# One TensorE increment per round in the routed stage, with the down product a round later

## What is computed

```python
xn = _layernorm(x, axis=-1)
x = x + _L0_attn_ref(xn, ...) + _L0_ffn_ref(xn, ...)

# the experts: 16 of them, each row goes to 6; H = 256, I = 176
topk_idx, topk_weight = _gate(hs, gate_weight, bias)
comb = zeros((T, E)).at[arange(T)[:, None], topk_idx].add(topk_weight)
for e in range(E):
    g = hs @ gate_proj[e].T
    u = hs @ up_proj[e].T
    inter = silu(g) * u
    out = out + comb[:, e:e + 1] * (inter @ down_proj[e].T)
# and a shared expert that every row goes to
```

## Time and profile before

| | us |
|---|---|
| median of 3 timed runs | 474.18 |
| lowest and highest | 473.19, 474.95 |
| span of the profiled execution (its own time; no time around it is recorded) | 518.7 |
| TensorE, VectorE, ScalarE, GpSimd busy in it | 426.0, 359.5, 228.7, 225.0 |
| gate/up products, 444 records | 156.4 |
| down products, 444 records | 117.3 |

### The profile page before, as it was taken

One profiled execution on the slowest core, in us unless ns is written; L12 is line 12 of the kernel. 1 busy time (PEld: TensorE's weight loads), 2 busy tenths in 40 slices (PEclk: granted clock), 3 DMA queues, 4 the chain that ended last, 5 costly groups with the idle time before them and its releaser, 6 DMA issues.

```text
span 518.7 us, 7330 instructions
## 1 busy us (share of the span) xinstructions
PE 426.0 (82%) x1981; PEld 324.8 (63%) x1981; DVE 359.5 (69%) x582; ACT 228.7 (44%) x614; POOL 225.0 (43%) x221
## 2 busy tenths in 40 slices
PE   6699986984979899898998999994987299979800
PEld 5698875764846667676776777673755177657600
DVE  3548931288698889898999999995630055548961
ACT  3542423211754444644576656632652044624400
POOL 2700175665346667671000000074757624466662
PEclk8559988898999999999999999998997689988955
DMA  7999925564725556567732333364567454464473
GB/s 201 345 351 396 385 104 177 176 245 153 225 66 190 174 189 192 167 195 211 191 106 88 102 106 109 102 176 124 155 178 191 123 149 141 133 174 142 122 219 89
DMA packets 65957, 91.55 MB, mean 176 GB/s; under 512 B 8448, under 2 KB 57344, under 8 KB 65664
## 3 DMA queue, kind: packets, MB, share of 16 engines
q1 hardware_dynamic: 54144, 63.02, 39.6%
q0 software_dynamic: 9216, 25.96, 16.2%
q10 hardware_dynamic: 2560, 2.10, 1.5%
HBM read 43.48 MB, written 47.57 MB: 176 GB/s over the span
## 4 chain that ended last, share of the span: by engine, by line
PE 60%; DVE 12%; issue 10%; another core or an unknown queue 6%; ACT 5%; POOL 2%; DMA 2%; SPq 2%; DVEq 0%; POOLq 0%; ACTq 0%
PE gate L923 20%; PE ps_y L946 15%; PE ps_y L939 4%; PE up L913 4%; PE misc L822 3%; PE ps_y L882 3%; PE misc L793 2%; PE misc L973 2%; PE gate L860 2%; DVE prod L1021 2%; PE up L860 1%; SPq L402 1%; PE ps_y L822 1%; DVE inter_s L1432 1%
## 5 line engine op out<-in xcount | busy, mean ns | idle before, releaser
L923 PE MATMUL gate<-wrec,xgT 128*128 x444 | 156.4, 476 | 3.8 <-DVE inter_s L1432 2.7
L562 POOL DMA_INDIRECT xs_dram<-xrow,slot_i x96 | 105.5, 1099 | 72.1 <-DMA xs_dram<-xrow,slot_i 25.8
L946 PE MATMUL ps_y<-wrec,interT 88*128 x444 | 117.3, 387 | 0.1
L582 POOL DMA_INDIRECT gat<-y_dram,slot_i x50 | 54.1, 1083 | 141.5 <-DMA y_dram<-y_s 103.0
L1432 DVE SCALAR_TENSOR_TENSOR inter_s<-gate,xg,gate_s 128x176 f32<-128x176 f32 x111 | 43.6, 393 | 80.6 <-ACT gate_s L687 38.7
L923 PEld LDWEIGHTS gate<-wrec,xgT 128*128 128x128 f32 x444 | 78.5, 197 | 30.7 <-issue 7.9
L946 PEld LDWEIGHTS ps_y<-wrec,interT 88*128 88x128 f32 x444 | 76.8, 193 | 7.5 <-issue 0.9
L939 PE MATMUL ps_y<-ident,inter_s 128*88 128x128 f32 x222 | 43.1, 276 | 33.3 <-issue 16.1
L939 PEld LDWEIGHTS ps_y<-ident,inter_s 128*88 128x88 f32 x222 | 25.6, 124 | 70.9 <-issue 51.4
L707 ACT ACTIVATE y_s<-ps_y 128x256 f32<-128x256 f32 x108 | 41.4, 383 | 63.7 <-PE ps_y L946 39.2
L687 ACT ACTIVATE gate_s<-gate 128x176 f32<-128x176 f32 x111 | 35.5, 320 | 72.6 <-PE gate L923 52.1
(11 more groups left out here) (200 smaller groups left out, 666.6 us busy)
## 6 DMA issues: line engine op xcount, KB each, us to landing
xg<-xs_dram SPq DMA_DIRECT2D x111, 136.0 KB
y_dram<-y_s SPq DMA_DIRECT2D x111, 128.0 KB
xs_dram<-zrow SPq DMA_DIRECT2D x1, 9384.0 KB, 33.7
wrec<-wexp SPq DMA_DIRECT2D x14, 608.0 KB
xs_dram<-zrow SPq DMA_DIRECT2D x14, 408.0 KB
xn_dram<-xrow SPq DMA_DIRECT2D x8, 256.0 KB, 3.3
qkv<-xn_dram SPq DMA_DIRECT2D x8, 256.0 KB
xs_dram<-xrow,slot_i POOLq DMA_INDIRECT x96
```

Of the source, the lines that this page charges most:

```text
L562: nc.gpsimd.indirect_dma_start(xs_dram[0:DONE[max(d for d in DONE if d <= c)] * P, :], bass.IndirectOffsetOnAxis(slot_i[:, o:o + 1], 0), x ...
L582: nc.gpsimd.indirect_dma_start(places[place_of(n)][:, there:there + H], None, y_dram[0:DONE[max(d for d in DONE if d <= first)] * P, :], b ...
L923: last = nc.tensor.matmul(guA[t % 2][:, 0:2 * I], xgT[:, t % 2, k * P:(k + 1) * P], wrec[:, bass.ds(record + k * 2 * I, 2 * I)], start=(k ...
L946: last = nc.tensor.matmul(ps_y[:, t % 2 * 2 * H:t % 2 * 2 * H + H], interT[:, t % 2, k * P:(k + 1) * P], wrec[0:HALF, bass.ds(record + KT ...
```

## The change

TensorE's round is reordered to columns(t+2), down(t-4), middle(t-2), gate/up(t), and only the last instruction of the round increments a semaphore, the new `round_ps`. The down product is one round later; the results and their stores follow, so there is one more round. Everybody who waited for a piece waits for the end of the round in which it stands (`rounds`). The buffers' other waits change with the order: the middle transposes wait for the middle copy of two tiles before in place of the result copy, the down product waits for the result copy of two tiles before, and VectorE's `middle` no longer waits for TensorE's transposes.

```diff
+        def rounds(t, later):
+
+            return t + later + 3
...
-            for t in range(NT + 3):
+            for t in range(NT + 4):
                 if t + LEAD < NT:
                     load_tile(t + LEAD)
-                if t >= 3:
-                    store_tile(t - 3)
+                if t >= 4:
+                    store_tile(t - 4)
...
-                act.wait_ge(xt_ps, t + 1)
+                act.wait_ge(round_ps, rounds(t, -2))
...
-                act.wait_ge(gu_ps, t + 1)
+                act.wait_ge(round_ps, rounds(t, 0))
...
-                act.wait_ge(it_ps, t + 1)
+                act.wait_ge(round_ps, rounds(t, 2))
...
-                if t + 2 in EXP_AT and t:
-                    act.wait_ge(y_sb, t)
-                act.wait_ge(yt_ps, t + 1)
+                if t + 3 in EXP_AT:
+
+                    act.wait_ge(it_sb, t + 3)
+                    if t:
+                        act.wait_ge(y_sb, t)
+                act.wait_ge(round_ps, rounds(t, 4))
...
-                    pe.wait_ge(y_sb, t - 1)
+                    pe.wait_ge(it_sb, t - 1)
...
                 pe.wait_ge(it_sb, t + 1)
+                if t >= 2:
+
+                    pe.wait_ge(y_sb, t - 1)
...
-                    gate_up_tile(t, held[t])
+                if t + 2 < NT:
+                    last = columns(t + 2)
+                if t >= 4:
+                    last = down_tile(t - 4, held[t - 4])
                 if 2 <= t <= NT + 1:
-                    middle(t - 2)
-                if t >= 3:
-                    down_tile(t - 3, held[t - 3])
-                if t + 2 < NT:
-                    columns(t + 2)
+                    last = middle(t - 2)
+                if t < NT:
+                    last = gate_up_tile(t, held[t])
+
+                last.then_inc(round_ps, 1)
...
                 dve.wait_ge(gate_ok, t + 1)
-                if t >= 2:
-
-                    dve.wait_ge(it_ps, t - 1)
-
...
-                dve.wait_ge(yt_ps, t + 1)
+                dve.wait_ge(round_ps, rounds(t, 4))
+                dve.wait_ge(it_sb, t + 3)
...
                 if t in EXP_AT:
-                    if t >= 3:
-                        tile_result(t - 3)
+                    if t >= 4:
+                        tile_result(t - 4)
```

More of the change, by code:

```diff
@@ L317, in build @@
         d_ok, y_ok = sem("d_ok"), sem("y_ok")
-        xt_ps, xt_sb, gu_ps, gate_ok, mid_ok, it_ps, it_sb, yt_ps, y_sb = (
-            sem("xt_ps"), sem("xt_sb"), sem("gu_ps"), sem("gate_ok"), sem("mid_ok"), sem("it_ps"), sem("it_sb"),
-            sem("yt_ps"), sem("y_sb"))
+        round_ps, xt_sb, gate_ok, mid_ok, it_sb, y_sb = (
+            sem("round_ps"), sem("xt_sb"), sem("gate_ok"), sem("mid_ok"), sem("it_sb"), sem("y_sb"))
         step, sub_ok, exp_ok, att_ok, attx_ok = sem("step"), sem("sub_ok"), sem("exp_ok"), sem("att_ok"), sem("attx_ok")
@@ L758, in _ @@
                 else:
-                    if t >= 3:
-                        result(t - 3)
+                    if t >= 4:
+                        result(t - 4)
                     if t + 2 < NT:
@@ L913, in columns @@
                     last = nc.tensor.transpose(guB[t % 2][:, k * P:(k + 1) * P], xg[:, t % RING, k * P:(k + 1) * P], ident[:, :])
-                last.then_inc(xt_ps, 1)
+                return last
             def gate_up_tile(t, record):
@@ L924, in gate_up_tile @@
                                             wrec[:, bass.ds(record + k * 2 * I, 2 * I)], start=(k == 0), stop=(k == KT - 1))
-                last.then_inc(gu_ps, 1)
+                return last
             def middle(t):
@@ L939, in middle @@
                     last = nc.tensor.transpose(ps_y[0:HALF, o:o + P], inter_s[:, t % 2, k * HALF:(k + 1) * HALF], ident[:, :])
-                last.then_inc(it_ps, 1)
+                return last
             def down_tile(t, record):
                 pe.wait_ge(it_sb, t + 1)
+                if t >= 2:
+                    pe.wait_ge(y_sb, t - 1)
                 for k in range(2):
@@ L947, in down_tile @@
                                             wrec[0:HALF, bass.ds(record + KT * 2 * I + k * H, H)], start=(k == 0), stop=(k == 1))
-                last.then_inc(yt_ps, 1)
+                return last
             def transpose_attention(j):
@@ L982, in _ @@
                 qkv_job(n)
-            columns(0)
-            columns(1)
+            columns(0).then_inc(round_ps, 1)
+            columns(1).then_inc(round_ps, 1)
             pe.wait_ge(w_in, 16 * TAIL)
             pe.wait_ge(tail_in, 16)
-            for t in range(NT + 3):
+            for t in range(NT + 4):
                 if t < NT:
@@ L1437, in tile_columns @@
                 dve.wait_ge(xt_sb, t)
-                dve.wait_ge(xt_ps, t + 1)
+                dve.wait_ge(round_ps, rounds(t, -2))
                 nc.vector.tensor_copy(xgT[:, t % 2, :], guB[t % 2][:, 0:H]).then_inc(xt_sb, 1)
@@ L1444, in tile_middle @@
                     dve.wait_ge(it_sb, t)
-                dve.wait_ge(it_ps, t + 1)
+                dve.wait_ge(round_ps, rounds(t, 2))
                 nc.vector.tensor_copy(interT[:, t % 2, :], ps_y[0:HALF, t % 2 * 2 * H + H:(t % 2 + 1) * 2 * H]).then_inc(it_sb, 1)
```

## The result

The changed kernel takes 483.21 us (median of 4 runs, 481.09 to 483.32), the kernel before 474.56 us (4 runs, 473.19 to 475.79). The ratio is 1.0175, 95% interval 1.0136 to 1.0213. The forecast of 474.8 us and its range to 480.0 were both too low. Every ratio in this document leaves out executions over 1.5% above the fastest of their kernel (one of some 1049 us of the kernel before on each of two chips, and one of 511.11 us with LEAD = 5, among them), while the medians of the experiments hold all.

The account below looks back on a forecast made before the run. TensorE was taken as the bound, with VectorE second and co-limiting from 250 to 346 us. The terms gave 474.18 + 0.44 (order) + 1.0 (exponentials) - 0.8 (fewer increments) = 474.8 us, range 466.5 to 480.0.

Parts of the forecast that it names:

- the room between a transfer's issue and its use: Loads of xg: 3.45 us until the column transposes, above known landings of 2.4 and 3.3 us; cost 0.
- Fewer signals: Three increments fewer per round: three quarters of the long rounds' excess gone, 31 us profiled, 0.8 us timed.
- a profile's own time: Span 518.7 us against timed 474.18; 41.0 us of long rounds read as belonging almost wholly to the profiled execution.

Follow-up runs that it names:

- LEAD = 5: Changed kernel with xg tiles loaded five rounds ahead in place of four; 526.79, 522.23 and 477.67 us, ratios 1.0166, 1.0065 and 1.0068 to the kernel before.
- four increments: Changed kernel's order, but a semaphore increment for each of TensorE's four pieces; 526.03 and 479.84 us, ratios 1.018 and 1.0106 to the kernel before.
- the changed kernel on chip 8: Changed kernel run again beside the kernel before on a chip of the quicker kind; 481.74 us against 474.52, ratio 1.014.

## What to carry to other kernels

When a change shortens the room between a transfer's issue and its use, compare the smallest room of any round, not that of a quiet one, with the longest landing beside the other traffic, not with a median or with another transfer, and ask what stands behind the waiting instruction: here it was the whole round of the engine that bounds. If the buffers allow it, issue one step earlier in the same change. Fewer signals were no gain here, where the producer never waited for them; waiting for the last of four pieces delays the work on the first three. And where a profile's own time is far from the timed ones, find out whether it comes from another chip before any of its stalls is priced.

## What the runs showed of the hardware that was not expected

- Chips of two kinds: medians of 474.2 to 474.6 us or 517.4 to 518.9 us for one and the same kernel. Why they differ stays open.
- On the slower kind ScalarE waited up to 7.4 us for a piece of TensorE's that had already ended, while GpSimd issued indirect transfers. With the gathers left out rounds 88 to 92 take 16.0 us there in place of 35 to 36. Sending a quarter of the signals did not help.
- Loads of the same 136 KB landed after 2.2 to 5.5 us within one execution, median 2.6; after 2.1 to 3.9 us in a kernel that has no gathers and loads a round earlier.
- A pause of 2.73 us of TensorE was followed by four us at a granted clock near 0.6, so that this late load cost 1.7 times its wait. Pauses of 1.43 us (four increments) and 1.03 us (the changed kernel on chip 8), both for the same tile, were not followed by a longer round.
